# Two batches share the expert slots of a hybrid transformer's last layer, and a list scheduler is re-tuned

## The reference

```python
x = x + attn_a(ln(x)); x = x + ffn(ln(x)); x = x + attn_b(ln(x)); x = x + ffn(ln(x))
x = x + attn_padded(ln(x))
x = x + experts(ln(x))          # "moe1"
x = x + attn_sink(ln(x))        # "sink"
x = x + experts(ln(x))          # "moe2"

def experts(x):                 # E = 8 experts, top K = 2, DM = 128, DE = 352
    y = rmsnorm(x, rms_w)
    vals, idx = top_k(y @ gate_w.T, 2)
    w = softmax(vals)
    h = silu(y @ W1[e].T) * (y @ W2[e].T)
    return x + sum over the two experts of w * (h @ W3[e].T)
```

## Time and profile before

| | |
|---|---|
| time, median of 3 runs | 2377.61 us (2374.21 to 2381.48) |
| the profiled execution's own time | 2365.46 us |
| its span, first to last instruction | 2363.7 us |
| instructions | 62948 |
| PE busy | 2149.6 us, 91% |
| DVE busy | 1641.8 us, 69% |
| ACT busy | 1422.7 us, 60% |
| POOL busy | 674.2 us, 29% |

### The profile page before, as it was taken

The page is one execution under the profiler, slowest core; times in us unless marked ns, Lnnn a source line. Parts: engine busy times, 40 slices in busy tenths (PEclk is TensorE's granted clock), DMA queues, the critical chain, the costliest instruction groups (busy, mean ns, idle before and its releaser), DMA issues.

```text
span 2363.7 us, 62948 instructions
## 1 busy us (share of the span) xinstructions
PE 2149.6 (91%) x26220; PEld 1224.9 (52%) x26243; DVE 1641.8 (69%) x3685; ACT 1422.7 (60%) x2105; POOL 674.2 (29%) x602
## 2 busy tenths in 40 slices
PE   7788988898999999899999999999999999999987
PEld 3222232223224233334554566697766887777987
DVE  9998879998876683423453388468687776866755
ACT  1367766666786889998777745644455234444333
POOL 4400000012002001203224214355515555424553
PEclk9999999999999999999999999999999999999998
DMA  6701100101121112112313324465624675634776
GB/s 189 222 18 35 41 17 17 44 17 50 27 50 45 25 34 65 51 23 68 92 47 87 78 48 113 106 204 158 184 50 117 188 222 168 192 101 123 229 240 195
DMA packets 160746, 235.23 MB, mean 100 GB/s; under 512 B 21968, under 2 KB 81872, under 8 KB 160208
## 3 DMA queue, kind: packets, MB, share of 16 engines
q1 hardware_dynamic: 145456, 206.81, 31.5%
q0 software_dynamic: 9984, 20.73, 2.5%
q10 hardware_dynamic: 5024, 3.67, 0.6%
HBM read 156.28 MB, written 73.88 MB: 97 GB/s over the span
## 4 chain that ended last, share of the span: by engine, by line
PE 56%; DVE 14%; ACT 11%; issue 7%; POOL 6%; DMA 5%; SPq 1%; POOLq 0%; DVEq 0%; ACTq 0%
PE PS L1205 16%; ACT PT L1367 10%; PE PS L1185 8%; DVE MS L1609 7%; PE PS L1154 5%; PE PS L1254 5%; DMA scr_y<-XN,SL 3%; PE PS L1141 3%; PE PS L1271 3%; PE PS L1054 2%; PE PS L1044 2%; POOL scr_o L1848 2%; PE PS L1015 2%; POOL scr_y L1840 2%; PE PS L1215 2%
## 5 line engine op out<-in xcount | busy, mean ns | idle before, releaser
L1367 ACT ACTIVATE PT<-PS 128x1024 f32<-128x1024 f32 (+5 forms) x1200 | 1018.6, 911 | 392.8 <-PE PS L1185 378.8
L1609 DVE TENSOR_REDUCE MS<-PS 128x2 f32<-128x1024 f32 (+3 forms) x736 | 778.2, 1097 | 141.4 <-PE PS L1154 136.1
L1205 PE MATMUL PS<-PT,VA 128*9 128x512 f32 (+7 forms) x6720 | 558.8, 434 | 14.3 <-ACT PT L1367 12.0
L1185 PE MATMUL PS<-QO,KO 64*64 64x512 bf16 (+7 forms) x6240 | 420.0, 305 | 47.0 <-ACT PT L1367 29.6
L1185 PEld LDWEIGHTS PS<-QO,KO 64*64 64x64 bf16 (+2 forms) x6240 | 177.5, 105 | 271.6 <-ACT PT L1367 130.9
L1154 PE MATMUL PS<-KO,QO 61*64 61x512 bf16 (+2 forms) x3520 | 286.4, 326 | 34.0 <-DVE MS L1609 16.6
L1254 PE MATMUL PS<-SG,WB 128*128 128x128 f32 x2208 | 276.1, 278 | 6.2 <-DMA WB<-in_mW 2.9
L1254 PEld LDWEIGHTS PS<-SG,WB 128*128 128x128 f32 x2208 | 261.8, 194 | 12.1 <-issue 7.3
L1154 PEld LDWEIGHTS PS<-KO,QO 61*64 61x64 bf16 (+1 forms) x3520 | 126.1, 104 | 243.4 <-DVE MS L1609 127.3
L1848 POOL DMA_INDIRECT scr_o<-SG,TO x184 | 182.0, 989 | 226.6 <-ACT SG L1402 197.4
L1205 PEld LDWEIGHTS PS<-PT,VA 128*9 128x9 f32 (+2 forms) x6720 | 127.8, 90 | 177.0 <-issue 115.4
(11 more groups left out here) (182 smaller groups left out, 2474.7 us busy)
## 6 DMA issues: line engine op xcount, KB each, us to landing
WB<-in_mW SPq DMA_DIRECT2D x184, 384.0 KB
PT<-scr_y SPq DMA_DIRECT2D x40, 264.0 KB, 4.6
PT<-scr_o SPq DMA_DIRECT2D x16, 512.0 KB, 5.3
QO<-scr_q_full SPq DMA_DIRECT2D x32, 192.0 KB
KO<-scr_k_full SPq DMA_DIRECT2D x32, 192.0 KB
QO<-scr_q_causal SPq DMA_DIRECT2D x32, 192.0 KB
QO<-scr_q_local SPq DMA_DIRECT2D x32, 192.0 KB
QO<-scr_q_padded SPq DMA_DIRECT2D x32, 192.0 KB
```

The costliest lines, as they stand in the source:

```text
L1185: p = mm(pb[c:c + n, h2, at:at + tn], k[:, k0 + c:k0 + c + n], q[:, t0:t0 + tn], start=not masked, stop=True, skip_group_check=masked)
L1205: p = mm(bank[32 * h:32 * h + D + 1, c0:c0 + tn], va[0:n, :], pt[0:n, plane, at:at + tn], start=s["first"] and j == 0, stop=s["last"] and ...
L1367: e = activation(pt[0:r, 0:n, a:b], ps[0:r, 0:n, a:b], ACT.Exp, scale=s["A"].scale)
L1609: v.tensor_reduce(to, got, AX.X, ALU.max).then_inc(S["top"], 1)
```

## The change

In moe1 each batch keeps 23 tiles of its own. In moe2, batches 0 and 1 share one set of slots: 2 x 16 + 7 = 39 tiles, where 2 x 23 = 46 stood; batches 2 and 3 keep 23 each. `tiles_of(n)` is 16 n + 7, and `GROUPS` names the sets. `routed` is the first half of the old `experts`, once per batch; `experts` is now the tiles, once per set; `combined` is the end, once per batch.

The second batch of the set keeps its own norm and ranks but must start them behind the first batch's (`others`). Its slots begin in the gaps that the first batch's rounding left and go on in tiles of its own behind the first one's. That takes further small DVE operations in `ranks`; the first batch of the set leaves four small copies (`KEEP`). `slot_load` of the set waits for the 16 scatters of both batches, and `rows_in` of both batches for all 39 tiles. The table of owners of tiles is 40 long for 24, in all sets. The buffer of batch 0 that is cleared early (`zero`) has 39 tiles for 23, that of batch 1 stays at 23.

The planner loses the shared line of transfers; each transfer has one fixed time to landing. PE costs of `up` and `down` go from 1340 to 1385 and from 670 to 755, and `product` gets 30 per block. `LEADS`, `URGENT`, `SHORT` and `WORTH` all have new values, so that the steps of all layers come in another order on every engine. The diff, cut to its core:

```diff
-SLOT_TILES, GROUP, ROW = 23, 4, 132
+GROUP, ROW, MOST = 4, 132, 39
+GROUPS = dict(moe1=((0,), (1,), (2,), (3,)), moe2=((0, 1), (2,), (3,)))
+def tiles_of(n):
+    return 16 * n + 7
...
-LEADS = dict(..., sink=(60610, 10946, -47942, -4076), moe2=(-46608, -58920, -16653, -27602))
+LEADS = dict(..., sink=(67712, 83703, -41855, 71689), moe2=(-19771, -96121, 7800, -25589))
...
-            for name, n, ns, moved in step.dmas(step):
+            for name, n, ns in step.dmas(step):
                 step.signals["dma"].name = name
-                self.moving = max(self.moving, at) + moved
-                self.due(step.signals["dma"], 16 * n, self.moving + ns)
+                self.due(step.signals["dma"], 16 * n, at + ns)
...
+    def experts(two, stage, slots, placed):
+        tiles, p = tiles_of(len(two)), two[0]
...
-load = add("slot_load", ... ("y_in%s_%s" % (b, t // GROUP), 1, 2900, 900)
+load = add("slot_load", ... ("rows_in%s" % s.use["pt"].i, 1, 5600)
-wl = add("weights", ... ("w_in%s" % s.use["wb"].i, 1, 1900, 1400)
+wl = add("weights", ... ("w_in%s" % s.use["wb"].i, 1, 4700)
-back = add("back", ... ("back%s" % s["yt"].i, 1, 2000, 50)
+back = add("back", ... ("back%s" % s["yt"].i, 1, 3600)
-scatter ... ("y_out%s" % b, 2, 1500, 100)
+scatter ... ("y_out%s" % b, 2, 4300)
-got = add("rows_in", ... ("g_in%s_%s" % (b, c), 1, 3000, 1850)
+got = add("rows_in", ... ("rows_in%s" % s.use["pt"].i, 1, 6300)
-zero ... [("sp", 6000, "")] ... ("zeroed%s" % b, 1, 15000, 0)
+zero ... [("sp", 500, "")] ... ("zeroed%s" % b, 1, 13000)
-s = add("ranks", [("pe", 238, "ranks_mm"), ("dve", 2950, "slots")], dict(top=[top]), ...
+s = add("ranks", [("pe", 238, "ranks_mm"), ("dve", 4200 if i else 2950, "slots")], dict(top=[top], others=others[1:]), ...
...
+    for stage, name in enumerate(STAGES):
+        for p, two in enumerate(GROUPS[name]):
+            slots, placed = [], []
+            for b in two:
+                slots, also = batches[b].send(slots)
+                placed += also
+            returned = experts(two, stage, slots[1:], placed)
+            for b in two:
+                batches[b].send(returned)
```

More of the change, by code:

```diff
@@ L122, in __init__ @@
         self.banks = {}
-        self.look, self.lead, self.coming, self.mode, self.moving = {}, 0, {e: 0 for e in ENGINES}, "whole", 0
+        self.look, self.layer, self.coming, self.mode = {}, None, {e: 0 for e in ENGINES}, "whole"
     def given(self, name, value, at):
@@ L142, in add @@
         attention = step.given.get("A")
-        step.lead = self.lead + 1000 * URGENT.get(step.kind + "_" + attention.name if attention else step.kind, 0)
+        step.name, step.layer = step.kind + "_" + attention.name if attention else step.kind, self.layer
+        step.lead = 1000 * (LEADS[step.layer[0]][step.layer[1]] if step.layer else 0) + 1000 * URGENT.get(step.name, 0)
         self.steps.append(step)
@@ L152, in look_ahead @@
             if step.dmas:
-                step.far += sum(ns + moved for name, n, ns, moved in step.dmas(step))
+                step.far += sum(ns for name, n, ns in step.dmas(step))
             step.far += max([far.get(s, 0) for s in step.signals.values()], default=0)
@@ L163, in urgency @@
         stays = engine == "pe" and step.mode[0] == self.mode
-        return short, step.far + step.lead + WORTH * stays, -step.index
+        changed = CHANGED.get(now // STRETCH, {})
+        return short, step.far + step.lead + 1000 * (changed.get(step.name, 0) + changed.get(step.layer, 0)) + WORTH * stays, -step.index
     def go(self, step, i, now):
@@ L796, in experts @@
             placed = []
-            for i in range(NT):
-                placed.append(add("scatter", [("pool", 2210, "")], dict(slots=slots, y=normed, zero=zeroed, landed=placed[-1:]), b=b, i=i, xn=xn,
-                                  dmas=lambda s: [("y_out%s" % b, 2, 1500, 100)])["dma"])
+            for j in range(NT):
+                placed.append(add("scatter", [("pool", 2210, "")], dict(slots=slots, y=normed, zero=zeroed, landed=placed[-1:]), b=b, p=p, i=j, xn=xn,
+                                  dmas=lambda s: [("y_out%s" % b, 2, 4300)])["dma"])
@@ L833, in experts, with combined @@
-            prev = [x["with_h"]]
+            return [normal] + slots, placed, wt, [x["with_h"]]
+        def combined(stage, returned, wt, prev):
+            two = [two for two in GROUPS[STAGES[stage]] if b in two][0]
             for c in range(2):
-                got = add("rows_in", [("sp", ISSUE, "")], dict(rows=returned), dict(pt=PT), b=b, c=c, dmas=lambda s, c=c: [("g_in%s_%s" % (b, c), 1, 3000, 1850)])
+                got = add("rows_in", [("sp", ISSUE, "")], dict(rows=returned), dict(pt=PT), b=b, p=two[0], c=2 * two.index(b) + c, dmas=lambda s: [("rows_in%s" % s.use["pt"].i, 1, 6300)])
@@ L872, in streams @@
     s.use["bank"].give(s["mbd"])
-    for b in range(NB):
-        batch(b)
+    batches = [batch(b) for b in range(NB)]
+    for b in batches:
+        next(b)
+    for stage, name in enumerate(STAGES):
[4 more added lines that the diff above has]
+                placed += also
+            plan.layer = (name, two[0])
+            returned = experts(two, stage, slots[1:], placed)
+            for b in two:
+                plan.layer = (name, b)
+                batches[b].send(returned)
 PACKS = dict(first=("ident", "wbd", "wvT", "wvb", "outT"),
```

257 lines of the change are left out of this document (160 added, 97 removed).

## The result

The changed kernel takes 2401.29 us (median, 2392.87 to 2402.90); the kernel before, run beside it, 2374.21 (2371.14 to 2381.48). The ratio is 1.0095, 95% interval 1.0081 to 1.0110: 0.95% slower, about 23 to 27 us. The forecast of 2355 had the sign wrong, and the time lies above its range. The profiled execution of after has a span of 2399.2 us. That of before had 2363.7 and lay 12 us under its median, so the two traces differ by 35.5 us where the medians differ by 27.

What follows compares the result with a forecast made beforehand. PE was taken to bound the kernel, busy 2149.6 of 2363.7 us. From the profiled 2365.5, 14.8 and 8 us came off; carried to the median, 2377.6 - 22.8 = 2354.8, rounded to 2355, range 2327 to 2394.

Steps and rivals of the forecast that it cites:

- part 2: What the pairing adds in moe2, including a first `slot_load` waiting for 16 landings instead of 8: taken as nothing.
- rival (b): Paired slots stay 194 us apart, so moe2 tiles no longer cover sink attention: slower, 2395; chance 0.18.
- part 1: Seven moe2 tiles less, mostly where PE is 88 to 98% busy: 14.8 us faster, bounds 0 and 14.8.
- The bound of 0: Lower bound for removing seven moe2 tiles: holes get longer by as much as was removed, so nothing is gained.
- Part 2's other terms: In `ranks`, some 15 more small DVE operations, 3.1 us, and longer tables, at most 1.5: taken as nothing.
- Part 3: The planner's later landings and costs cut waits on PE: between 0 and 22.0 us gained, 8 taken.
- The other sign: Second test of the planner's new times: PE over 92 in the window of 2200 to 2300.
- Part 4: All other steps re-ordered by new leads and urgencies: 0 taken, 15 us allowed to either side.
- The frame: The first 700 us were given nothing; the prediction is wrong in its frame if the time moves there.
- (d): Rival: the new order closes most holes, 42 us faster, 2336; chance 0.22.
- The rule weighed there: Interleaving regimes may gain; a pairing that makes the fifth set's tiles wait takes that away, costed as rival (b).

Runs made afterwards that it cites:

- the pairing alone: Batches 0 and 1 paired in moe2 in before's order with before's landings, against before: 2396.41 us beside 2377.34, ratio 1.0070.
- the wait-alone run: Before's order, all 46 tiles, no pairing; batch 0's moe2 slot loads also wait for batch 1's scatters, against before: 2405.38 us, ratio 1.0108.
- The control: The changed kernel's code with no pairing and before's planner times and order, against before: 2430.71 us beside 2427.51, ratio 1.0006.

## Why the prediction was wrong

**The step that failed is in part 2: the first `slot_load` that waits for 16 landings was put at nothing, and rival (b), cover lost, got a chance of 0.18.** That the second batch's chain of scatters "was there before" is true, but batch 0's 23 tiles did not wait for it before. The wait by itself costs 26 to 28 us. Rival (b) had mechanism and place right, and its price close. It gave 2395, ends 2378 and 2412; measured were 2401.3, and 2396.4 for the pairing alone. It should have been the forecast. Its own test was met: the pair's second slots came after 2050, at 2166.97, and PE was under 90 from 2050 to 2150 (86.6). Fifteen tiles more than before stood behind 2150; it had said sixteen (23 less 7). It gave the emptier stretch 0 to 33.9 us of shrinking; the pairing alone shows about 17 at the last slots. Its middle is that good in part by luck: it was chosen as the middle of an open range.

What the prediction held against (b) was that the new leads of sink "are the largest for batches 0 and 1". They are not: batch 3's is 71.7, above batch 0's 67.7. And a lead is one term of the planner's ranking and no time. It was read as if the batches came in the order of their numbers, and the order 0, 2, 1, 3 wasn't looked for. The trace of before held the answer: the fifth and sixth sets of slots are 194 us apart, so any partner of the fifth had to come 134 us earlier (1980 for 2113.89) to meet the prediction's own test for part 1. The emptied stretch gives 56 us of that (138 for 194 in the pairing alone).

**Part 1 was mis-sized where it was placed.** The price of a tile, 2.12 us, holds: seven of them in the last set bring 14 to 18 us. Seven of batches 0 and 1 bring none (1.0011), where 14.8 was taken. The bound of 0, holes that get longer by as much as was removed, is what came. Four of the seven were cover for the last batch's scatters. The three of batch 0 stood where PE is 98% busy, and they too moved no slots that the traces can show, though nineteen of the same batch bring over half of their price. So "98% leaves little room" was too strong, and how much a tile is worth there is between nothing and some half of its price. With the wait added, the same seven tiles are worth about 9 us, as they now stand behind the last slots.

**Part 2's other terms**, nothing for the pairing's own small operations: none of the runs shows them by themselves, and none needs them.

**Part 3 had the waits right and the value wrong.** L1423's waits for `scr_o` fell under 15 us (8.0), as foretold. On the chips where before takes 2374 to 2377 us, they are 22.1 to 40.7 us in the eight traces with before's landings and 5.2 to 8.2 in the three with after's. But these waits didn't carry 8 us of the end. Where before's order was kept they fell as much, and the time rose by 44 us; and on the slower chip before's own order shows 5.4 us of them. The other sign, the window of 2200 to 2300 over 92 (97.1), came true by luck: the pairing alone, with the old landings, has 92.8 there, since tiles were moved into it. As for the 44 us, the step `scatter` waits in the middle of its chain, and putting other steps ahead can turn a wait of POOL into a later scatter. That this is what happened is argued and not shown; shown is that the last slots came 50 us later.

**Part 4** was left at 0, plus or minus 15. The whole change costs 1.0095 (1.0081 to 1.0110), the pairing in before's order 1.0070 (1.0046 to 1.0093). So parts 3 and 4 together cost about 0.25%, 6 us, and by the intervals it may be nothing. That they hang together (1.0186 and 1.0190 when one is exchanged without the other) wasn't foreseen.

**The frame** held. In the first 100 us the clock is 0.86 for 0.98 in after and the first unit's `QO<-MTd` transfer goes out 10 us later (92.46 for 82.77), but both kernels are nearly level at 2000 us (668 and 672 score reductions, 1096 and 1128 `up` matmuls, which is under three tiles). Of the sum, one slip: the lower bound of (d) with part 4 is 2377.6 - 14.8 - 22.0 - 15 = 2325.8 and not 2327.

**The rule weighed there.** The Trainium skill (Perfetto Trace Analysis, Optimization Strategy) says that interleaving stretches with different most-contended engines may help. The runs bear it out by taking it back: with tiles and sink attention apart, the wait-alone run loses 1.08%.

What stays open: how much of the 0.25% is the landings and how much the order; and what a single tile of batch 0 is worth, since seven tiles of batches 0 and 1 and nineteen of batch 0 were measured on different chips, where before differs by 2%. A run in which after's own planner makes the order for single sets wasn't made; its tables lead to an order that its own clock puts 38 us later than after's.

## What to carry to other kernels

That an engine is 98% busy does not say what work taken off it brings: here the same seven tiles' worth brought nothing in one place and its full price in another. Ask what the removed work covers. Behind the last piece of real input, find how long that input's own chain takes; other work counts only as far as it is longer than that chain. Before two work items are merged so as to save rounding, read from the trace when each of them becomes ready, in their order in time and not in the order of their numbers; the merged one is ready with the later. And where a planner's model of times is corrected, its order has to be found anew, and fewer waits in the trace are no sign that the end comes sooner.

## What the runs showed of the hardware

The same kernel took 2374 to 2377 us on three chips and 2427.5 on a fourth, 2.2% more. The control's trace, before's order on that chip, stands for it beside the trace of before. The groups are nearly as long (the `up` group 280.2 for 276.1 us at the same count). PE's busy time is 28.5 us longer in all, and its idle time before `down` is 43.9 us for 16.8. The granted clock of all runs of before doesn't part the chips: 0.979 to 0.985 on this one, 0.979 to 0.988 on one of the others. What makes the difference stays open. So only ratios to the kernel before on the same chip are compared here.

The granted clock was 0.93 in 2050 to 2150 of after, where PE is busy for 86.6 of 100 us, and 1.00 in 2200 to 2300, where it is busy for 97.1. The kernel without matmuls on NOTHING shows 0.95 in 2000 to 2100 at 81.7 us busy, after 0.97 at 89.8, and the time of the two is the same.
